# Expert stage of a fused attention and mixture-of-experts kernel: outputs scaled a turn later, low weights split on VectorE, scatters a tile later

## The reference

```python
probs = softmax(xn @ router_w.T)
w = top_p_weights(probs, 0.9)
for e in range(8):
    g = silu(xn @ gate_w[e].T)          # 256 -> 512
    u = xn @ up_w[e].T
    y = g * u @ down_w[e].T             # 512 -> 256
    out = out + y * w[:, e:e + 1]
return x + attention(xn) + out
```

## Time and profile before

| | us |
|---|---|
| median of 3 runs | 926.46 (923.11 to 931.77) |
| the profiled execution | 922.48 |
| its span, first to last instruction | 920.8 |

### The profile page before, as it was taken

One profiled execution on the slowest core, in us unless ns is written; L12 is line 12 of the kernel. 1 busy time (PEld: TensorE's weight loads), 2 busy tenths in 40 slices (PEclk: granted clock), 3 DMA queues, 4 the chain that ended last, 5 costly groups with the idle time before them and its releaser, 6 DMA issues.

```text
span 920.8 us, 21143 instructions
## 1 busy us (share of the span) xinstructions
PE 789.1 (86%) x7104; PEld 718.4 (78%) x7105; DVE 573.1 (62%) x1262; ACT 347.0 (38%) x770; POOL 402.2 (44%) x397
## 2 busy tenths in 40 slices
PE   5889898898989897388898887988987989889993
PEld 5767677676767676388898887988987979888993
DVE  5788787878786957645556465455555565565442
ACT  3133333333424252344344443343443443443441
POOL 3010101010101015546667577576657566676663
PEclk9899999999999997689999999999999999999997
DMA  3111120202020204212524335324325324333332
GB/s 116 70 47 51 42 87 5 92 0 92 0 92 0 70 2 150 52 36 44 123 47 80 93 47 121 51 46 126 53 40 120 52 46 115 52 52 58 58 58 35
DMA packets 38419, 57.99 MB, mean 63 GB/s; under 512 B 4096, under 2 KB 33792, under 8 KB 37376
## 3 DMA queue, kind: packets, MB, share of 16 engines
q0 software_dynamic: 19776, 27.16, 18.4%
q1 hardware_dynamic: 18624, 30.59, 9.6%
HBM read 35.58 MB, written 22.15 MB: 63 GB/s over the span
## 4 chain that ended last, share of the span: by engine, by line
PE 33%; DVE 24%; issue 16%; DMA 10%; ACT 9%; POOL 4%; ACTq 2%; POOLq 1%; DVEq 1%
DMA out<-ybuf,s_idx 7%; PE A L1040 6%; PE A L1042 6%; PE A L1041 6%; DVE h L1021 4%; DVE s_sb L764 4%; PE S L1078 3%; ACT h_hi L692 3%; DVE h_lo L1023 3%; DMA xg<-gather_table,g_idx 3%; PE O L1040 2%; PE O L1042 2%; PE O L1041 2%; PE O L1105 1%; ACT sg L690 1%
## 5 line engine op out<-in xcount | busy, mean ns | idle before, releaser
L373 POOL DMA_INDIRECT out<-ybuf,s_idx x104 | 173.8, 1671 | 59.7 <-POOL s_idx L461 42.7
L1040 PE MATMUL A<-gT_hi,w_hi 128*128 128x256 f32 x588 | 168.4, 286 | 4.7 <-issue 3.2
L1023 DVE TENSOR_TENSOR h_lo<-h,h_hi 128x256 fp32r<-128x256 f32 x196 | 110.0, 561 | 94.8 <-ACT h_hi L692 94.8
L1041 PE MATMUL A<-gT_lo,w_hi 128*128 128x256 f32 x588 | 167.1, 284 | 0.0
L1042 PE MATMUL A<-gT_hi,w_lo 128*128 128x256 f32 x588 | 166.9, 284 | 0.0
L1040 PE MATMUL O<-w_hi,h_hi 128*128 128x256 f32 x392 | 119.5, 305 | 19.1 <-DVE h_lo L1023 19.1
L356 POOL TENSOR_TENSOR kf<-kz 128x256 f32<-128x256 f32 x16 | 18.9, 1184 | 257.8 <-DVE kz L759 257.8
L448 POOL DMA_INDIRECT xg<-gather_table,g_idx x100 | 100.6, 1006 | 62.1 <-POOL g_idx L446 43.2
L692 ACT ACTIVATE h_hi<-h 128x256 fp32r<-128x256 f32 x196 | 81.9, 418 | 109.5 <-DVE h L1021 109.5
L1040 PEld LDWEIGHTS A<-gT_hi,w_hi 128*128 128x128 f32 x588 | 113.8, 194 | 6.6 <-issue 6.5
L1041 PEld LDWEIGHTS A<-gT_lo,w_hi 128*128 128x128 f32 x588 | 113.5, 193 | 0.0
(11 more groups left out here) (181 smaller groups left out, 1641.0 us busy)
## 6 DMA issues: line engine op xcount, KB each, us to landing
w_raw<-wffn SPq DMA_DIRECT2D x8, 1536.0 KB, 6.5
gather_table<-xna SPq DMA_DIRECT2D x8, 528.0 KB
xa<-x SPq DMA_DIRECT2D x8, 512.0 KB, 3.5
xr<-x SPq DMA_DIRECT2D x8, 512.0 KB, 4.8
out<-yout SPq DMA_DIRECT2D x8, 512.0 KB
out<-ybuf,s_idx POOLq DMA_INDIRECT x104, 3.9
xg<-gather_table,g_idx POOLq DMA_INDIRECT x100
w_raw<-wqk_nat SPq DMA_DIRECT2D x1, 512.0 KB, 5.2
```

The costliest lines, as they stand in the source:

```text
L373: pool.indirect_dma_start(out=out, out_offset=bass.IndirectOffsetOnAxis(ap=s_idx[:, sub:sub + 1], axis=0), in_=ybuf[:, sub, :], in_offset= ...
L1023: v.tensor_tensor(h_lo[:, ic, :], h[:, ic, :], h_hi[:, ic, :].bitcast(F32), ALU.subtract).then_inc(hlo_ok, 1)
L1040: mm(out_ap, l_hi, r_hi, start=(k == 0), stop=False)
L1041: mm(out_ap, l_hi, r_lo, start=False, stop=False)
```

## The change

- Outputs a and b leave the end of a turn. In turn t they stand between chunk 1 and chunk 2 and write the outputs of tile t-1 (`outputs_a`, `outputs_b`); after the loop they run once more. Their routing weight's column is kept in a register from the turn before. One `pe.nop` signals the first `y_ps`.
- The scatter of tile n-3 now stands in POOL's turn n (`LAG` 3, three column registers, one more scatter after the loop). It copies `s_idx` before it waits for the outputs. `scattered` is split in two semaphores, one per half of `ybuf`, and each output write waits for its own.
- The low pieces move from POOL to DVE: two ahead of an expert's first tile and two behind it, as the high pieces on ACT are now too. The last expert, which had none, gets four of each, and SP loads its weights once more for them.
- The copy into `w_tok` moves from DVE to ACT, behind `gT_hi`.
- POOL waits for the last `yout` store ahead of its first gather and no longer ahead of each scatter.
- An expert has at least two tiles (`MIN_TILES`); with this data that adds none.

```diff
-LAG = 2
+MIN_TILES = 2
+LAG = 3
...
-            for e in range(2, NE):
+            for e in range(2, NE + 1):
                 next_weights(e)
...
             def scatter():
 
-                pool.wait_ge(yout_free, DMA * (NBLK + 1))
                 n = pool.snap(done)
-                pool.wait_ge(ya_ok, n + 1)
-                pool.wait_ge(yd_ok, n + 1)
-
-                pool.wait_ge(scattered, (n + 1) * (SUB * DMA))
+                pool.wait_ge(scattered_a, n * DMA)
+                pool.wait_ge(scattered_b, n * DMA)
                 pool.sem_inc(pool_gate, 1)
-                link(g.tensor_copy(s_idx[:, :], idx_all[:, bass.ds(pool.snap(col2, min_val=0, max_val=NE * (NT // P) - SUB), SUB)]))
+                link(g.tensor_copy(s_idx[:, :], idx_all[:, bass.ds(pool.snap(col3, min_val=0, max_val=NE * (NT // P) - SUB), SUB)]))
+                pool.wait_ge(ya_ok, n)
+                pool.wait_ge(yd_ok, n)
+                pool.sem_inc(pool_gate, 1)
                 add_rows()
 
+            pool.wait_ge(yout_free, DMA * (NBLK + 1))
             tiles = TileCounts(pool, n_tiles)
...
+            with pool.Fori(0, NE) as e:
+                n = tiles.now()
+                tiles.load_next(e + 1)
+                with pool.Fori(0, n) as j:
+                    col = pool.snap(e * (NT // P) + j * SUB)
+                    gather(col)
+                    with pool.If(pool.snap(done) > LAG - 1):
+                        scatter()
                     pool.sem_inc(pool_gate, 1)
-                    tiles.step()
+                    pool.reg_add(done, done, 1)
+                    pool.reg_mov(col3, col2)
+                    pool.reg_mov(col2, col1)
+                    pool.reg_mov(col1, col)
+                tiles.step()
...
             def tokens_hi(n):
 
                 act.wait_ge(xg_free, n + 2)
                 a.activation(gT_hi[:, :, :].rearrange("p c t -> p (c t)"), A[0][:, :], ACT.Copy).then_inc(ghi_ok, 1)
+                a.activation(w_tok[:, bass.ds(n * (SUB * NE), SUB * NE)].rearrange("p (a e) -> p a e", a=SUB),
+                             xg[:, :, D:AUG], ACT.Copy).then_inc(wt_ok, 1)
+
+            def outputs_a(t):
+
+                act.wait_ge(y_ps, t * SUB + 1)
+                act.wait_ge(scattered_a, (t + 2) * DMA)
+                c = act.snap(wcol, min_val=0, max_val=NE * MAX_TILES * SUB * NE)
+                a.activation(ybuf[:, 0, :], O[0][:, 0:D], ACT.Copy, scale=w_tok[:, bass.ds(c, 1)]).then_inc(ya_ok, 1)
+
+            def tile(e):
+
+                t = act.snap(done, min_val=0, max_val=NE * MAX_TILES - 1)
+                for ic in range(IC):
+                    act.wait_ge(gu_ps, t * IC + (ic + 1))
+                    a.activation(sg[:, ic, :], bank_gu(ic)[:, 0:FT], ACT.Silu).then_inc(silu_ok, 1)
+                    act.wait_ge(h_free, t * IC + (ic + 1 + IC))
+                    a.activation(h_hi[:, ic, :], h[:, ic, :], ACT.Copy).then_inc(hhi_ok, 1)
+                    if ic == 1:
+                        outputs_a(t)
+                tokens_hi(t + 1)
+                act.reg_mov(wcol, t * (SUB * NE) + e)
+                act.reg_add(done, done, 1)
...
+            def outputs_b(t):
+
+                dve.wait_ge(y_ps, t * SUB + 2)
+                dve.wait_ge(scattered_b, (t + 2) * DMA)
+                dve.wait_ge(wt_ok, t + 1)
+                c = dve.snap(wcol, min_val=0, max_val=NE * MAX_TILES * SUB * NE - NE)
+                v.tensor_scalar(ybuf[:, 1, :], O[1][:, 0:D], w_tok[:, bass.ds(c + NE, 1)], None, ALU.mult).then_inc(yd_ok, 1)
...
+                    for piece in range(PIECES // 2):
+                        low_piece(1 - par, piece * PW, ep * (2 * PIECES) + (PIECES * (par + 1) + 1 + piece))
+                    tile(ep * 2 + par)
+                    for piece in range(PIECES // 2, PIECES):
+                        low_piece(1 - par, piece * PW, ep * (2 * PIECES) + (PIECES * (par + 1) + 1 + piece))
+                    with dve.Fori(1, n):
+                        tile(ep * 2 + par)
                     tiles.step()
+            outputs_b(dve.snap(done, min_val=0, max_val=NE * MAX_TILES))
```

More of the change, by code:

```diff
@@ L249, in build @@
          gathered, xg_free, ghi_ok, glo_ok, gu_ps, silu_ok, h_free, hhi_ok, hlo_ok, y_ps, ya_ok, yd_ok,
-         wt_ok, scattered, pool_gate, dve_gate, pe_gate, act_gate, whi_ok) = [sems[n] for n in names.split()]
+         wt_ok, scattered_a, scattered_b, pool_gate, dve_gate, pe_gate, act_gate, whi_ok) = [sems[n] for n in names.split()]
         nat = w_raw[:, 0:2 * KC * D].rearrange("p (m c k) -> p m c k", m=2, c=KC)
@@ L370, in add_rows @@
             def add_rows():
-                for sub in range(SUB):
+                for sub, landed in enumerate((scattered_a, scattered_b)):
                     pool.indirect_dma_start(
                         out=out, out_offset=bass.IndirectOffsetOnAxis(ap=s_idx[:, sub:sub + 1], axis=0),
-                        in_=ybuf[:, sub, :], in_offset=None, compute_op=ALU.add).then_inc(scattered, DMA)
+                        in_=ybuf[:, sub, :], in_offset=None, compute_op=ALU.add).then_inc(landed, DMA)
             def add_zeros(n):
@@ L434, in _ @@
             col2 = pool.alloc_register("col2")
-            pieces = pool.alloc_register("pieces")
-            piece_col = pool.alloc_register("piece_col")
-            for r in (done, col1, col2):
+            col3 = pool.alloc_register("col3")
+            for r in (done, col1, col2, col3):
                 pool.reg_mov(r, 0)
@@ L503, in _ @@
             gather(0)
             scatter()
-            pool.reg_add(done, done, 1)
-            pool.reg_mov(col2, col1)
-            scatter()
-            pool.reg_add(done, done, 1)
-            pool.wait_ge(scattered, (pool.snap(done) + 1) * (SUB * DMA))
+            for older, newer in ((col2, col1), (col1, col1)):
+                pool.reg_add(done, done, 1)
+                pool.reg_mov(col3, older)
+                pool.reg_mov(col2, newer)
+                scatter()
+            pool.wait_ge(scattered_a, (pool.snap(done) + 1) * DMA)
@@ L511, in _ @@
+            pool.wait_ge(scattered_b, (pool.snap(done) + 1) * DMA)
         @block.scalar
@@ L643, in _ @@
             act.reg_mov(done, 0)
[L644 to L645 removed]
+            wcol = act.alloc_register("act_weight_col")
+            act.reg_mov(wcol, 0)
             def tokens_hi(n):
@@ L1007, in tokens_lo, with tile, low_piece @@
                                 gT_hi[:, :, :].rearrange("p c t -> p (c t)").bitcast(F32), ALU.subtract).then_inc(glo_ok, 1)
-                v.tensor_copy(w_tok[:, bass.ds(n * (SUB * NE), SUB * NE)].rearrange("p (a e) -> p a e", a=SUB),
-                              xg[:, :, D:AUG]).then_inc(wt_ok, 1)
+            def outputs_b(t):
[4 more added lines that the diff above has]
+                v.tensor_scalar(ybuf[:, 1, :], O[1][:, 0:D], w_tok[:, bass.ds(c + NE, 1)], None, ALU.mult).then_inc(yd_ok, 1)
+            def tile(e):
+                t = dve.snap(done, min_val=0, max_val=NE * MAX_TILES - 1)
+                for ic in range(IC):
+                    dve.wait_ge(silu_ok, t * IC + (ic + 1))
+                    v.tensor_tensor(h[:, ic, :], sg[:, ic, :], bank_gu(ic)[:, FT:2 * FT], ALU.mult).then_inc(h_free, 1)
+                    dve.wait_ge(hhi_ok, t * IC + (ic + 1))
+                    v.tensor_tensor(h_lo[:, ic, :], h[:, ic, :], h_hi[:, ic, :].bitcast(F32),
+                                    ALU.subtract).then_inc(hlo_ok, 1)
+                    if ic == 1:
+                        outputs_b(t)
+                tokens_lo(t + 1)
+                dve.reg_mov(wcol, t * (SUB * NE) + e)
+                dve.reg_add(done, done, 1)
+            def low_piece(par, c0, n):
+                dve.wait_ge(whi_ok, n)
+                whi = w_hi[par][:, bass.ds(c0, PW)]
+                v.tensor_tensor(w_lo[par][:, bass.ds(c0, PW)], w_raw[:, bass.ds(c0, PW)], whi.bitcast(F32),
+                                ALU.subtract).then_inc(wsplit, 1)
             tokens_lo(0)
```

113 lines of the change are left out of this document (19 added, 94 removed).

## The result

| | before | changed |
|---|---|---|
| median of 4 runs, us | 925.91 (923.11 to 931.77) | 1107.89 (1103.28 to 1108.71) |
| the profiled execution | 922.48 | 1108.71 |
| its span | 920.8 | 1107.0 |
| mean granted TensorE clock | 0.945 | 0.882 |

The ratio is 1.190, with a 95% interval of 1.184 to 1.196. The change makes the kernel slower by 182 us; the forecast was 1108, within 1080 to 1145.

What follows compares the result with a forecast made beforehand. PE, busy 86% of the span, bounded the old kernel; a one-tile scatter loop would rule the changed one. Span 920.8 + 3 + 167.4 + 6.4 + 5 = 1102.6, plus 1.7 outside and 4.0 to median: 1108 us, range 1080 to 1145.

Steps and rivals of the forecast that it cites:

- The loop: Expert stage from the fourth tile: output writes wait for a scatter behind the next gather; 14.05 us a tile, +167.4 us.
- Loads: Expert stage: each of 7 weight loads, asked for about 2.5 us after a G, costs 0.7 us; +5, bounds 0 and 20.
- Start: Stage start: yout wait moves G(0) by +6 us, tiles 0 to 2 give some 3 back; net +3.
- My last term: Whole run: the median of the runs shown lies 4.0 us above the profiled execution, so 4.0 is added.
- End: After G(49): two scatters follow, each after the one before has landed; 24.7 us instead of 18.3, +6.4.
- Low pieces: They leave POOL (28 × 2.39 us) and become 32 on DVE at 0.97 us each; cost taken 0.
- PE: Expert stage: PE's 9.0 us of work fits in 14.05, standing still some 5 us a tile; busy about 65%.
- Rival A: Expert stage: the scatter wait is covered and every tile runs at PE's 9.0 us; 871 us median, chance 0.07.
- Rival C: Expert stage: idle PE falls to the low clock and takes over at 15.0 us a tile; 1152 us, chance 0.07.
- Rival D: Expert stage: only the first scatter's landing counts, loop 1.93 us shorter at 12.1; 1019 us, chance 0.02.
- Rival B: Expert stage: new waits eat what POOL gains, no change, loop of about 10.4 us; 926 us, chance 0.02.

Runs made afterwards that it cites:

- three ways out: Three kernels, each the changed one with one order altered: scatter ahead of gather, LAG back at 2, or outputs at the turn's end; 901.78, 898.44 and 863.35 us.
- copy_twice: Changed kernel with POOL's copy into s_idx made twice between gather and scatter; 1125.12 us, step 14.61 us.
- load_late: Changed kernel with each of the stage's seven weight loads held until the gather under way has landed; 1123.53 us.
- low_twice: Changed kernel with every low piece made twice on DVE, 32 more pieces; 1116.68 us.
- outputs_end: Changed kernel with outputs back at the turn's end, behind gT and w_tok, and LAG 2; low pieces stay on DVE, w_tok on ACT; 863.35 us.
- lag_two: Changed kernel with LAG back at 2, so POOL's turn n scatters tile n-2; outputs stay in mid-turn, scatter behind the gather; 898.44 us.
- halves_reversed: Changed kernel with each scatter's halves issued in the other order, DVE's half b first, ACT's half a second; 1118.48 us.
- end_dve_wtok_plain: outputs_end with the w_tok copy back on DVE behind gT_lo, and no added wait for it ahead of ACT's output; 904.99 us.

## Why the prediction was right

The forecast's steps, against the profile of the changed kernel:

- **The loop.** Predicted 14.05, bounds 13.7 and 14.4; a quiet tile takes 14.02. G to DVE's write 10.61 (10.43 predicted): the waits that now stand between s_idx and the first scatter make the gap 1.01 instead of 0.87, as allowed for, and the landing takes 4.10. From the write to gT_hi 2.41 (2.49), gT_hi to w_tok 0.48 (0.58, the overlap), w_tok on ACT 0.21 (0.21), to G 0.31 (0.33). Errors of +0.2 and −0.2 cancelled. The experiments show both that it limits (three ways out) and its slope (copy_twice, 0.44 for 0.47).
- **Loads.** 0.7 us each, 5 in all. The 46 steps exceed 46 × 14.02 by 6.9 us. That looks like the forecast, but it isn't the loads: most of it stands in the experts' first tiles (14.5 to 14.9), and each load starts a tile later. I priced a gather held up by the load. That happens (transposes at G+9.2, where load_late has 7.1 to 7.8), and is hidden. The first half of the scatter lands 1 us late (ACT writes at G+9.8, not G+8.7), which is hidden too, since the second half, for which the loop waits, lands 3.9 to 4.2 us after its issue, as elsewhere. So a load costs next to nothing here; what could have cost much is the scatter, and low_twice and load_late show that it was near.
- **Start.** Predicted +3, measured +7.0, in three parts. The wait for the yout store is 3.9, not 6: G(0) stands 5.1 behind the store's issue, where I had 4.8 for its landing and some 2 more for the tile counts. Tiles 0 to 2 gave back 0.9, not 3: that step was wrong by 2. And the first stage, which the change doesn't touch, ended 4.0 later in this execution (store at 389.91, not 385.95). Over the 14 profiles that issue lies between 384.1 and 390.3, so it varies from run to run. My last term, +4.0 from profile to median, had another ground and was wrong by itself: the changed kernel's profiled execution is 0.8 above its median. It filled just the gap that the late first stage left, so the agreement of 1108 with 1107.89 is luck; by its own terms the span came out 4.4 short (1102.6 for 1107.0), which is still close.
- **End.** +6.4 predicted, +6.4 measured; the last issue is 20.93 after G(49), not 14.26.
- **Low pieces.** 0.97 us each predicted, 0.92 measured, and a cost of nothing; that cost was wrong. The 6.9 us above are mostly theirs. By my schedule no piece stood at a G; they run from G+0.4 to G+3.1, beside the gather's two instructions on POOL. The first tile of the last expert:

```profile
1005.53 0.19 POOL L448 COPY g_idx<-idx_all 128x2 uint32 x1 [5.86 <-ACT w_tok L632]
1006.46 1.83 DVE L1011 TENSOR_TENSOR w_lo<-w_raw,w_hi 128x768 fp32r<-128x768 f32 x2 [0.63 <-ACT w_hi L546]
1006.60 1.72 POOL L450 DMA_INDIRECT xg<-gather_table,g_idx  x1 [0.89 <-POOL g_idx L448]
...
1012.73 1.77 POOL L375 DMA_INDIRECT out<-ybuf,s_idx  x1 [0.30 <-issue]
```

  The gather's first instruction takes 1.72 us where it takes 1.03 in other tiles, and the second scatter is issued at G+7.20, not G+6.51. In the seven first tiles these issues are 0.5 to 0.7 late, 4.1 us together; in the tile behind each, one gather instruction takes 1.24 instead of 1.03, some 1.5 us more in all. So the pieces cost about 5.5 us, and the 5 us that I had put down for the loads came true only because two errors cancelled. DVE's own time is hidden, as I had said; POOL's is on the loop.
- **PE.** Busy 10.7 of 14.05 was predicted and measured at 10.74 of 14.00. The sentence that it would be busy some 65% of the stage, and stand still 5 us a tile, is wrong beside it: the low clock fills 1.7 of these 5 us, and 77% is busy.
- **Rival A** (871) would have come true without the loop: outputs_end measured 863. It took more than an earlier scatter, as lag_two shows. **Rival C** fell as argued: the clock does drop in every tile, to a mean of 0.88, and costs only slack. The Trainium skill (TensorE: Matmul & The Clock Gate, HAM oscillation) tells of a kernel that falls to half rate at each long wait for a DMA; here a gap of 3.28 us is followed by 0.72 over 4 us, so the trace agrees for a part of these 4 us. **Rival D** is refuted by halves_reversed. **Rival B** needed a loop of 10.4.

## What to carry to other kernels

With a buffer that exists once, count for each wait which issue of which turn it needs, and which instruction of which engine releases that issue; where the waiting instruction stands ahead of that release, the loop is closed over one tile, and its length can be summed from rows before anything is run. Move such a wait behind the instruction that releases the next transfer (here 245 us). And when a step moves on one engine, look where the large loads land against the small latency-bound transfers: a wait of 0.7 us for one instruction was worth 42 us in end_dve_wtok_plain.
